# Start of an attention and expert kernel: x loaded in four uneven parts, inverse roots as a power on GpSimd, TensorE kept occupied between batches

## What is computed

```python
x = x + cross_attention(layernorm(x), ctx, pos, Wq, Wkv, Wout, bout)   # 32 heads of 8, rotary positions on q and k
x = x + mixture(layernorm(x), gate, experts, shared)                   # 32 experts, 6 a token, 48 places each
layernorm(x) = (x - mean(x)) / sqrt(var(x) + 1e-5)
```

## Time and profile of the kernel before

| | |
|---|---|
| median of 3 runs | 368.56 us (367.84 to 369.81) |
| the profiled execution, whole | 369.8 us |
| span in its profile | 367.8 us |
| busy: PE, DVE, POOL, ACT | 86%, 60%, 53%, 51% of the span |
| mean TensorE clock granted | 0.956 of full speed |

### The profile page before, as it was taken

How to read it: one execution, slowest core, us unless ns; L and a number is a source line. 1 busy time by engine, 2 the same in 40 slices (tenths; PEclk the granted TensorE clock), 3 DMA queues, 4 the chain that set the end, 5 groups by cost and what they waited for, 6 DMA issues and landing times. The chain is left out here.

```text
span 367.8 us, 9525 instructions
## 1 busy us (share of the span) xinstructions
PE 315.5 (86%) x3094; PEld 218.1 (59%) x3094; DVE 221.8 (60%) x621; ACT 188.2 (51%) x389; POOL 196.3 (53%) x285
## 2 busy tenths in 40 slices
PE   0668999999999999999998558889999989999930
PEld 0445777777777777777676324445765764555520
DVE  4466777676777666777777445788549044454520
ACT  4153668767668767668667375271344342233310
POOL 5569876667866667866200181053788411525460
PEclk9996999999999999999999858999999999999985
DMA  6511114454454454543210033203123275953446
GB/s 169 183 37 30 31 25 116 119 149 118 136 138 115 116 148 115 146 132 87 77 46 3 0 115 111 69 0 87 46 84 105 67 219 181 295 136 44 52 50 228
DMA packets 33292, 37.93 MB, mean 103 GB/s; under 512 B 7808, under 2 KB 27568, under 8 KB 33200
## 3 DMA queue, kind: packets, MB, share of 16 engines
q1 hardware_dynamic: 22610, 22.03, 20.6%
q10 hardware_dynamic: 8030, 11.93, 11.7%
q0 software_dynamic: 2624, 3.61, 5.9%
HBM read 26.36 MB, written 8.96 MB: 96 GB/s over the span
## 5 line engine op out<-in xcount | busy, mean ns | idle before, releaser
L405 ACT ACTIVATE pw<-bank 128x512 f32<-128x512 f32 x128 | 78.0, 615 | 53.3 <-PE bank L635 45.1
L496 DVE TENSOR_REDUCE mx<-bank 128x4 f16<-128x512 f32 x128 | 86.2, 684 | 9.6 <-PE bank L611 8.2
L624 PE MATMUL bank<-qst,kz 128*128 128x128 f16 x512 | 50.3, 221 | 0.3 <-ACT pw L405 0.2
L611 PE MATMUL bank<-kz,qst 128*128 128x512 f16 x128 | 49.6, 389 | 0.9 <-DMA kz<-kT 0.9
L624 PEld LDWEIGHTS bank<-qst,kz 128*128 128x128 f16 x512 | 36.0, 98 | 14.6 <-issue 6.8
L943 POOL DMA_INDIRECT acc<-ac,dst x16 | 23.5, 1471 | 35.3 <-ACT ac L1025 23.4
L264 POOL TENSOR_TENSOR t<-qk,RC 128x512 f32<-128x512 f32 x15 | 19.1, 1272 | 40.2 <-ACT qk L416 40.2
L503 DVE COPY mxs<-bank 8x128 f16<-8x128 f16 x64 | 13.4, 210 | 36.4 <-PE bank L615 36.4
L635 PE MATMUL bank<-pw,V 128*32 128x128 f32 x1024 | 34.6, 276 | 0.0
L1245 PE MATMUL mbank<-hT,WSG 128*128 128x512 f16 (+1 forms) x144 | 32.0, 379 | 0.0
L635 PEld LDWEIGHTS bank<-pw,V 128*32 128x32 f32 x1024 | 26.0, 109 | 7.3 <-issue 5.0
(11 more groups left out here) (192 smaller groups left out, 640.2 us busy)
## 6 DMA issues: line engine op xcount, KB each, us to landing
ring_gu<-in_L_ffn_w_gate_up ACTq DMA_DIRECT2D x20, 352.0 KB
kz<-kT SPq DMA_DIRECT2D x64, 64.0 KB, 2.0
ring_dn<-in_L_ffn_w_down ACTq DMA_DIRECT2D x10, 352.0 KB
ring_gu<-in_L_ffn_w_gate_up SPq DMA_DIRECT2D x8, 352.0 KB
X<-in_x SPq DMA_DIRECT2D x4, 512.0 KB, 8.1
table<-ac SPq DMA_DIRECT2D x8, 256.0 KB, 2.2
acc<-X SPq DMA_DIRECT2D x4, 512.0 KB, 3.7
out<-acc SPq DMA_DIRECT2D x4, 512.0 KB, 5.6
```

Source lines behind the costliest of these rows:

```text
L405: act.activation(pw[g % 4][:, :], STB[g % 2][:, :], ACT.Exp, scale=SCALE).then_inc(exp_ok, 1)
L496: dve.tensor_reduce(mx[u // 2 % 2][:, u % 2:8:2], SB[u % 2][:, :].rearrange("p (j t) -> p j t", j=4), axis=AX.X, op=ALU.max, negate=True). ...
L611: pe.matmul(SB[u % 2][:, :], qst[m.par][:, u, :], kz[m.par][:, :, u, :], start=True, stop=True).then_inc(s_mm, 1)
L624: ins = pe.matmul(STB[g % 2][:, j * P:j * P + P], kz[m.par][:, j, g, :], qst[m.par][:, g, :], start=True, stop=True)
```

## The change

It does the following:

- x is loaded as batch 0, batches 1 to 3, 4 to 9 and 10 to 15. WKV is loaded in two halves, its first half (keys) ahead of WQ. Its second half (values), BO and WO go to the end, behind all of x, on one semaphore (bo_in, 48). The context of batch 1 is still issued after all of them.
- ACT's square root and DVE's reciprocal are replaced by one `tensor_tensor` of POOL that raises (variance + EPS) to the power -0.5. `statistics` and `factors` are now two functions, called for batch 0, batches 1 to 3, and 4 to 15.
- POOL clears kz after the first normalising on ACT (xn_ok, 1), ahead of its wait for the loads; it takes the power for batches 4 to 15 at the head of period -1, behind rotation and split of batch 1.
- PE no longer waits for the weights first. It runs 30 products of the identity with 256 columns whose results nobody reads (`keep_warm`), 4 more after the transposing of batch 0, 18 after its projections, and 6 after those of batch 1.

```diff
@@ -35,6 +35,7 @@
+XPART = [0, 1, 4, 10, NB]
@@ -297,13 +299,15 @@
-                sp.dma_start(X[:, 4 * c:4 * c + 4, :], xr[:, 4 * c:4 * c + 4, :]).then_inc(x_in[c], 16)
+                part = slice(XPART[c], XPART[c + 1])
+                sp.dma_start(X[:, part, :], xr[:, part, :]).then_inc(x_in[c], 16)
                 if c == 0:
                     sp.dma_start(CT[0][:, :], ctx_in[0]).then_inc(ctx_in_s[0], 16)
+                    sp.dma_start(WKV[:, 0:D], wkv[:, 0:D]).then_inc(w_in, 16)
                     sp.dma_start(WQ[:, :, :], wq.rearrange("(c p) n -> p c n", p=P)).then_inc(w_in, 16)
-                    sp.dma_start(WKV[:, :], wkv).then_inc(w_in, 16)
-                    sp.dma_start(WO[:, :, :], wout.rearrange("(c p) n -> p c n", p=P)).then_inc(w_in, 16)
-                    sp.dma_start(BO[:, :], bout.rearrange("(a n) -> a n", a=1).broadcast_to([P, D])).then_inc(bo_in, 16)
+            sp.dma_start(WKV[:, D:], wkv[:, D:]).then_inc(bo_in, 16)
+            sp.dma_start(BO[:, :], bout.rearrange("(a n) -> a n", a=1).broadcast_to([P, D])).then_inc(bo_in, 16)
+            sp.dma_start(WO[:, :, :], wout.rearrange("(c p) n -> p c n", p=P)).then_inc(bo_in, 16)
@@ -356,14 +360,25 @@
-            pool.wait_ge(bo_in, 16)
+            pool.memset(power[:, :], -0.5).then_inc(consts, 1)
+            pool.wait_ge(consts, 7)
+
+            def spread(a, e, k):
+                pool.wait_ge(mv1_ok, k + 1)
+                pool.tensor_tensor(rs1[:, a:e, 0], nb1[:, a:e, 0], power[:, a:e], ALU.pow).then_inc(rs1_ok, 1)
+
+            spread(0, 1, 0)
+            pool.wait_ge(xn_ok, 1)
+            for i in range(2):
+                pool.memset(kz[i][:, :, :, :].rearrange("p j q t -> p (j q t)").bitcast(F32), 0.0).then_inc(kz_zero, 1)
+            spread(1, 4, 1)
+            pool.wait_ge(bo_in, 48)
 
             def period(b):
+                if isinstance(b.n, int) and b.n == -1:
+                    spread(4, NB, 2)
                 if inside(b + 3):
                     add_bias(b + 3)
-                    if isinstance(b.n, int) and b.n == -3:
-                        for i in range(2):
-                            pool.memset(kz[i][:, :, :, :].rearrange("p j q t -> p (j q t)").bitcast(F32), 0.0).then_inc(kz_zero, 1)
@@ -378,13 +393,8 @@
-            def std(a, e, k):
-                act.wait_ge(mv1_ok, 2 * k + 2)
-                act.activation(rs1[:, a:e, 0], nb1[:, a:e, 0], ACT.Sqrt).then_inc(std1, 1)
-            std(0, 4, 0)
-
             def norm(m):
-                act.wait_ge(rs1_ok, 2 if isinstance(m.n, int) and m.n < 4 else 4)
+                act.wait_ge(rs1_ok, 6 if not isinstance(m.n, int) or m.n > 3 else 4 if m.n else 2)
@@ -405,7 +415,7 @@
-                        act.wait_ge(consts, 6)
+                        act.wait_ge(consts, 7)
@@ -426,8 +436,6 @@
-                    if g == 4 and isinstance(b.n, int) and b.n == -1:
-                        std(4, NB, 1)
@@ -462,30 +470,30 @@
-                    if j % 4 == 0:
-                        dve.wait_ge(x_in[j // 4], 16)
+                    if j in XPART:
+                        dve.wait_ge(x_in[XPART.index(j)], 16)
                     dve.bn_stats(st1[:, j, :], X[:, j, :]).then_inc(stat1, 1)
                 for j in range(a, e):
-                    dve.wait_ge(stat1, j + 1)
+                    dve.wait_ge(stat1, j + k + 1)
                     ins = dve.bn_aggr(mv1[:, j, :], st1[:, j, :])
-                ins.then_inc(mv1_ok, 1)
-                dve.wait_ge(mv1_ok, 2 * k + 1)
+                ins.then_inc(stat1, 1)
+                dve.wait_ge(stat1, e + k + 1)
                 dve.tensor_scalar(nb1[:, a:e, 0], mv1[:, a:e, 1], EPS, None, ALU.add).then_inc(mv1_ok, 1)
-                if k == 0:
-
-                    dve.wait_ge(sin_s, 1)
-                    sin = ang[:, 0].rearrange("p b a f -> p b (a f)")
-                    cos = ang[:, 1].rearrange("p b a f -> p b (a f)")
-                    for r in range(2):
-                        dve.tensor_copy(RC[:, :, :, r], cos)
-                        dve.tensor_scalar(RS[:, :, :, r], sin, -1.0 if r == 0 else 1.0, None, ALU.mult).then_inc(rope_tab, 1)
-                dve.wait_ge(std1, k + 1)
-                dve.reciprocal(rs1[:, a:e, 0], rs1[:, a:e, 0]).then_inc(rs1_ok, 1)
+
+            def factors(a, e, k):
                 dve.wait_ge(rs1_ok, 2 * k + 1)
...
 
-            statistics(0, 4, 0)
+            statistics(0, 1, 0)
+            factors(0, 1, 0)
+            dve.wait_ge(sin_s, 1)
+            sin = ang[:, 0].rearrange("p b a f -> p b (a f)")
+            cos = ang[:, 1].rearrange("p b a f -> p b (a f)")
+            for r in range(2):
+                dve.tensor_copy(RC[:, :, :, r], cos)
+                dve.tensor_scalar(RS[:, :, :, r], sin, -1.0 if r == 0 else 1.0, None, ALU.mult).then_inc(rope_tab, 1)
+            statistics(1, 4, 1)
@@ -551,9 +559,11 @@
+                        factors(1, 4, 1)
                         split(dve, m3)
                     if g == 7 and isinstance(b.n, int) and b.n == -2:
-                        statistics(4, NB, 1)
+                        statistics(4, NB, 2)
+                        factors(4, NB, 2)
@@ -598,6 +608,8 @@
+                if isinstance(m.n, int) and m.n == 0:
+                    pe.wait_ge(bo_in, 48)
@@ -655,7 +667,12 @@
-            pe.wait_ge(w_in, 48)
+            def keep_warm(n):
+
+                for i in range(n):
+                    pe.matmul(OB[1][:, 0:2 * P], identh[:, :], identf[:, :].bitcast(F16), start=True, stop=True)
+
+            keep_warm(30)
@@ -673,6 +690,9 @@
+                        if isinstance(b.n, int) and b.n == -3:
+                            keep_warm(4)
+                            pe.wait_ge(w_in, 32)
@@ -685,6 +705,8 @@
+                        if isinstance(b.n, int) and b.n < -1:
+                            keep_warm(18 if b.n == -3 else 6)
```

More of the change, by code:

```diff
@@ L209, in attention @@
         rs1 = sb("rs1", [P, NB, 1])
+        power = sb("power", [P, NB])
         nb1 = sb("nb1", [P, NB, 1])
@@ L225, in attention @@
         mx_zero = sem("mx_zero")
-        stat1, mv1_ok, std1, rs1_ok = sem("stat1"), sem("mv1_ok"), sem("std1"), sem("rs1_ok")
+        stat1, mv1_ok, rs1_ok = sem("stat1"), sem("mv1_ok"), sem("rs1_ok")
         turn_s, sin_s, rope_tab = sem("turn_s"), sem("sin_s"), sem("rope_tab")
```

## The result

| | median | runs |
|---|---|---|
| before | 370.17 us (365.94 to 373.56) | 22 |
| changed | 371.98 us (369.48 to 375.03) | 22 |

Ratio 1.0075, 95% interval 1.0047 to 1.0104: slower by 0.75%, some 2.8 us. The forecast was no change, 368.5 us in a range of 365.7 to 370.9. (With 22 runs the median of before itself is 1.6 us above the 368.56 of the first three.)

The account below looks back on a forecast made before the run. PE sets the pace once the pipeline runs, so only the start counted: -1.05 (clock and context) + 1.2 (handoff) = 0.15 us, rounded to 0, hence 368.5 us against the median; range 365.7 to 370.9.

Parts of the forecast that it names:

- The power's price: POOL's power for the inverse roots: taken as 0.3 us, between 0.10 and 0.72 from rows of other POOL operations.
- the handoff: POOL's power ahead of DVE's first row maximum: maximum 8.9 us behind `project_q` instead of 7.72, costing 1.2 us (1.0 to 1.6).
- The mechanism: Before the first row maximum, DVE waits for POOL's power behind batch 1's rotation and split; the delay reaches the end whole.
- the power is dear: Slower rival: POOL's power of 12 columns costs 1.6 us, maximum 2.6 later, 371.1 us in all; chance 0.14.
- The product: DVE's product behind POOL's power, ahead of the first row maximum: taken as 0.3 us, between 0.16 and 0.61.
- the 0.4 I put beside the sum: If DVE's product waited out POOL's addition of BO (0.72), the sum would be 0.4 us worse; not included.
- Batch 0 earlier, worth nothing: PE begins batch 0 at 8.0 to 8.9, 0.9 to 1.8 us earlier; no gain, since batch 1 needs its context.
- The clock and the context, -1.05: Batch 1 up to the end of `project_q`: possible high clock and context 0.15 earlier gain 0.15 to 1.95, taken as 1.05 us.
- The context at 15.6: Batch 1's context, still last in the load queue, lands at about 15.6 us as before.
- the first rival: Load queue runs dry earlier, at 13.4; first maximum at 25.1, 2.8 us earlier, 365.8 us in all; chance 0.22.

Follow-up runs that it names:

- e4: The kernel before with one part of the change alone, POOL's power for the inverse roots of batches 4 to 15: ratio 1.0100 against before.
- e1: The changed kernel with the inverse roots of batches 4 to 15 back on ACT's square root and DVE's reciprocal: ratio 1.0045 against before.
- g4: The changed kernel with all inverse roots on ACT and DVE, no power on POOL: ratio 0.9999 against before.
- e5: The changed kernel with DVE's product for batches 4 to 15 moved behind the first row maxima, power kept on POOL: ratio 0.9970 against before.
- second look: The changed kernel, unedited, profiled and measured again: ratio 1.0060 against before.
- g2: Repeat of the changed kernel with the inverse roots of batches 4 to 15 on ACT and DVE: ratio 1.0020 against before.
- e3: The changed kernel with the context of batch 1 issued right behind batches 1 to 3 of x: ratio 1.0022 against before.
- e6: The changed kernel with batch 1's context issued early and DVE's product for batches 4 to 15 moved behind the first row maxima: ratio 0.9880 against before.
- e8: The changed kernel with batch 1's context issued early and the inverse roots of batches 4 to 15 on ACT and DVE: ratio 0.9951 against before.
- f1: The changed kernel with early context and late product, without the six extra products after batch 1's projections: ratio 0.9894 against before.

## Why the prediction was wrong

- **The power's price is the step that failed.** "I take 0.3, nearer to the short one, as it has 1 to 12 columns." It took 0.59 us for 1 column, 0.87 for 3 and 2.27 for 12, which a line of about 0.44 + 0.15 a column fits. Both ends of my bound, 0.10 and 0.72, came from simple operations, and the power of 12 columns, the one in the sum, lies far above both. The term of the sum, +1.2 for the handoff, measured +3.2 (10.98 - 7.74). The power alone is 1.97 of the 2.0 us more. The rest nearly cancels: the product, below, held the maximum 0.3 longer than forecast (0.61 from its start), and the power started 8.05 behind q instead of 8.21.
- **The mechanism was right.** POOL's path decides, `row_max` stands behind DVE's wait, and what the distance loses reaches the end (e4: 3.3 us of distance, 3.7 by the ratio). The rival "the power is dear" was what happened. Its 371.1 is 2.6 above the forecast's median of before, against 2.8 measured, but that nearness is partly luck: its power of 1.6 us was also too short, and 0.9 of its 2.6 came from a low clock for batch 1, which only some of the profiles show. The chance of 0.14 was too small for a price that no row gave.
- **The product.** The Trainium skill, SBUF — State Buffer, section "SBUF: two separate sides", would have it wait out POOL's addition. It took 0.69 us (31.44 to 32.13), ending with the addition of 0.72 that had started just before it (31.38 to 32.10). In e1 the product started first and took 0.17. Trace and rule agree, and the 0.4 I put beside the sum belonged in it.
- **Batch 0 earlier, worth nothing:** right. PE at 7.97 for a forecast of 8.0 to 8.9, and no gain shows while the context of batch 1 comes last (g4, 0.9999).
- **The clock and the context, -1.05:** not confirmed in size. Power alone is 1.0100 and all of the change 1.0060 to 1.0075, so that 0.9 to 1.5 us would come back, but the intervals overlap; +3.2 for the handoff and 2.8 for the whole leave only 0.4; and g4, with before's distance, shows no gain (0.9999, within 1.8 us either way). In the profiled execution the term had the wrong sign, q 0.92 later. In single profiles of the changed kernel and its variants the clock stood high for batch 1 (e1, e5, g4), fell during it (second look, g2) or just before it (first).
- **The context at 15.6:** it landed between 14.5 and 15.6 with the old order (four profiles) and between 14.3 and 16.6 with the new one, so the queue did not run dry earlier, and nowhere by the 13.4 of the first rival, which falls.

## What to carry over

- A tiny operation handed to another engine costs its own time plus all that is queued ahead of it there, and everything behind the wait pays. Put the wait where the result is needed: moving one call made the kernel 3 to 4 us faster with the power still in place.
- A price for which the trace has no row of the same operation is not bounded by rows of simpler ones. Put the upper end far off, and give the case in which it is reached a chance to match.
- Before speeding up the first step, ask what the second waits for. Here a load at the end of the queue made 1.8 us worthless. With it moved, and the extra products kept, `project_q` of batch 1 ran at the high clock in all four profiles (e3, e6, e8, f1).

## What was not expected of the hardware

DVE's addition of EPS for three columns took 2.57 us, where the one of four columns had taken 0.17. It ran from 8.98 to 11.55, exactly until POOL's clearing of kz ended (7.98 + 3.55 = 11.53). The Trainium skill, SBUF — State Buffer, section "Who interferes with whom", says that such a VectorE operation can enter a mode that needs the port pair shared with GpSimd, and that whoever comes second is blocked for the whole instruction; the rows fit that in the main. The addition started anywhere from 8.96 to 10.06 in the profiles of the changed kernel and its variants, and in 12 of 13 it ended within 0.04 us of the end of the clearing, whenever it had started. The clearing is two instructions of 1.80 us, though, so an addition that starts at 8.98, in the first, waits for the second as well. In the 13th (g4) it ended with the first of them:

```profile
7.97 3.54 POOL L373 MEMSET kz<- 128x2048 f32 x2 [0.89 <-ACT xn L397]
...
10.06 1.48 DVE L482 TENSOR_SCALAR nb<-mv 128x3 f32<-128x3 f32 x1
```

```profile
8.55 3.57 POOL L365 MEMSET kz<- 128x2048 f32 x2 [2.86 <-ACT xn L393]
...
9.51 0.87 DVE L478 TENSOR_SCALAR nb<-mv 128x3 f32<-128x3 f32 x1
```

The first pair is e1, the second g4 (8.55 + 1.81 = 10.36, and 9.51 + 0.87 = 10.38). Why the addition got in between there and not elsewhere is open. In before, where POOL clears kz only from 12.00, the addition of four columns took 0.17 at 7.42; no run moved the clearing alone to test the cause. In the changed kernel the wait is hidden; with the early context the clearing, this addition and the power of three columns behind it are what batch 1 waits for at 13.38.
